# A message ring of 19 pairs filled from the last score on, fewer statistics operations per pair, group 2 normalised inside the sums, two limit loads for four

## The reference

```python
h = relu(layernorm(x))
x_src, x_dst = h @ W_src.T, h @ W_dst.T
alpha = sum(x_src[src] * att_src[type]) + sum(x_dst[dst] * att_dst[type])   # per edge and head, self loops of type 0 added
alpha = where(alpha >= 0, alpha, 0.2 * alpha)
a = exp(alpha - segment_max(alpha, dst)[dst])
a = a / segment_sum(a, dst)[dst] * edge_weight
out = segment_sum(x_src[src] * a, dst) + bias
g = layernorm(out + h) * ln1_g + ln1_b
ff = gelu(g @ ffn_W1.T + ffn_b1) @ ffn_W2.T + ffn_b2
return x + layernorm(g + ff) * ln2_g + ln2_b
```

## Time and profile before

| | us |
|---|---|
| median of 3 runs | 3229.35 (3222.22 to 3236.22) |
| the profiled execution | 3217.3 |
| its span, first to last instruction | 3215.6 |

### The profile page before, as it was taken

The page is one execution under the profiler, slowest core; times in us unless marked ns, Lnnn a source line. Parts: engine busy times, 40 slices in busy tenths (PEclk is TensorE's granted clock), DMA queues, the critical chain, the costliest instruction groups (busy, mean ns, idle before and its releaser), DMA issues.

```text
span 3215.6 us, 56979 instructions
## 1 busy us (share of the span) xinstructions
PE 2992.1 (93%) x19965; PEld 2730.3 (85%) x19965; DVE 2254.3 (70%) x6326; ACT 1802.3 (56%) x3372; POOL 1729.2 (54%) x1493
## 2 busy tenths in 40 slices
PE   4887365999999999999999999999999999999998
PEld 4776344999999998999999999999999999999997
DVE  6888654777777776777777767777777777777775
ACT  4676243555555555555555555555555555555554
POOL 5665654555555555555555555555555555555552
PEclk9999687999999999999999999999999999999999
DMA  4446283222111222222222222221211122222210
GB/s 153 139 146 132 64 234 85 60 60 58 54 55 58 59 59 59 60 60 60 60 60 60 60 60 60 60 58 55 56 57 58 58 58 60 60 60 60 60 47 27
DMA packets 86991, 228.73 MB, mean 71 GB/s; under 512 B 19367, under 2 KB 23501, under 8 KB 86706
## 3 DMA queue, kind: packets, MB, share of 16 engines
q1 hardware_dynamic: 53810, 145.86, 13.3%
q0 software_dynamic: 31664, 78.07, 11.6%
q10 hardware_dynamic: 1232, 1.15, 0.1%
HBM read 146.85 MB, written 78.20 MB: 70 GB/s over the span
## 4 chain that ended last, share of the span: by engine, by line
PE 81%; DVE 1%; POOL 1%; issue 1%; ACT 1%; DMA 0%; DVEq 0%; POOLq 0%; ACTq 0%
PE ps_f L1324 33%; PE ps_a L1339 12%; PE ps_a L1341 11%; PE ps_a L1340 11%; PE ps_x L1361 8%; PE ps_t L1371 3%; PE ps_t L1349 3%; ACT h L715 0%; DVE arena L1129 0%; DVE act_lo L1189 0%; POOL arena L610 0%; POOL n_rstd L586 0%; ACT ps_f L740 0%; DMA arena<-sums,node_rows 0%; DVE arena L1155 0%
## 5 line engine op out<-in xcount | busy, mean ns | idle before, releaser
L1189 DVE TENSOR_TENSOR act_lo<-ps_f,act_hi 128x512 fp32r<-128x512 f32 x784 | 539.2, 688 | 742.6 <-ACT ps_f L740 742.3
L739 ACT ACTIVATE act_hi<-ps_f,hidden_bias 128x512 fp32r<-128x512 f32 x784 | 537.0, 685 | 863.6 <-PE ps_f L1324 863.6
L1339 PE MATMUL ps_a<-ffn_hi,act_hi 128*128 128x256 f32 x3136 | 900.5, 287 | 2.8 <-DVE arena L1155 2.7
L1341 PE MATMUL ps_a<-ffn_hi,act_lo 128*128 128x256 f32 x3136 | 887.5, 283 | 0.0
L1340 PE MATMUL ps_a<-ffn_lo,act_hi 128*128 128x256 f32 x3136 | 884.7, 282 | 0.0
L1324 PE MATMUL ps_f<-zt_hi,ffn_hi 128*128 128x512 f32 x1568 | 617.9, 394 | 11.6 <-DVE act_lo L1189 9.9
L1339 PEld LDWEIGHTS ps_a<-ffn_hi,act_hi 128*128 128x128 f32 x3136 | 591.5, 189 | 31.4 <-issue 4.5
L1324 PE MATMUL ps_f<-zt_lo,ffn_hi 128*128 128x512 f32 x1568 | 616.9, 393 | 0.0
L1324 PE MATMUL ps_f<-zt_hi,ffn_lo 128*128 128x512 f32 x1568 | 616.9, 393 | 0.0
L1340 PEld LDWEIGHTS ps_a<-ffn_lo,act_hi 128*128 128x128 f32 x3136 | 591.0, 188 | 24.1
L1341 PEld LDWEIGHTS ps_a<-ffn_hi,act_lo 128*128 128x128 f32 x3136 | 590.9, 188 | 0.0
(11 more groups left out here) (230 smaller groups left out, 5436.3 us busy)
## 6 DMA issues: line engine op xcount, KB each, us to landing
xb<-in_x SPq DMA_DIRECT2D x98, 512.0 KB, 5.9
out<-arena SPq DMA_DIRECT2D x98, 512.0 KB, 5.0
msgs<-arena SPq DMA_DIRECT2D x49, 256.0 KB
arena<-msgs SPq DMA_DIRECT2D x49, 256.0 KB, 4.7
sums<-arena SPq DMA_DIRECT2D x49, 256.0 KB, 3.9
arena<-sums,node_rows POOLq DMA_INDIRECT x392, 3.7
xb<-in_x,arena POOLq DMA_INDIRECT x196, 2.8
arena<-in_w_t SPq DMA_DIRECT2D x2, 1024.0 KB, 7.5
```

What stands on the lines that cost most here:

```text
L739: act.activation(act_hi[:, m % AB, :], ps_f[:, m % 2, :], ACT.Gelu, bias=hidden_bias[:, m:m + 1]).then_inc(act_hi_ready, 1)
L1189: dve.tensor_tensor(act_lo[:, m % AB, :], ps_f[:, m % 2, :], act_hi[:, m % AB, :].bitcast(F32), ALU.subtract).then_inc(act_lo_ready, 1)
L1339: pe.matmul(to, act_hi[:, m % AB, cols], ffn2[0][:, m, :], start=(m == 0 and t % 2 == 0), stop=False, skip_group_check=True)
L1341: ins = pe.matmul(to, act_lo[:, m % AB, cols], ffn2[0][:, m, :], start=False, stop=(m == MF - 1), skip_group_check=True)
```

## The change

1. `front_stats`: the two DVE operations that made var + EPS and -mean are gone. The square root takes EPS as its bias, `front_rstd` adds EPS and turns the sign inside operations that were there. mv has four slots.
2. The ring in which messages wait for their store is MB = 4 pairs, not two.
3. The ring of messages loaded back is SB = 19 pairs, not 4. Four of its slots (SBN) are a place of their own; the other 15 (msg_late) lie over the scores' parts, base and the stored messages. SP issues 4 loads behind the last message store, 15 more when alpha_ready is there and all messages are stored, and then one per pair as its slot comes free.
4. Node groups: input_stats(0) stands in pair 47, input_stats(1) behind alpha_ready, input_stats(2) in pair 12 of the sums. n_var and n_mm have two slots. POOL's input_rstd of groups 0, 1 and 2 stands ahead of c = 8, 20 and 84. ACT's relu of group 2 stands in the sums, behind the equals of pair 26.
5. ACT issues a gelu of one column that nobody reads behind the Exp.
6. Fix: one load each from SP and ACT, first and last rows of half the chunks. POOL loads the node rows only when the first record is made (they lie elsewhere now).

The core of the diff:

```diff
-SB = 4
+MB = 4
+SB = 19
+SBN = 4
...
-RSTD_AT = (16, 24)
+RSTD_AT = (8, 20, 84)
+STATS2_AT = 12
+RELU2_AT = 26
...
-        assert (RB - 1) * NT <= NCH * SC
-        other_rows = src_sc.rearrange("p c s -> p (c s)")[:, 0:(RB - 1) * NT].bitcast(I32).rearrange("p (b t) -> p b t", b=RB - 1)
-        msg_out = part([2, 2, D])
+        msg_out = part([MB, 2, D])
...
+        msg_late = arena[:, edges_end:edges_end + (SB - SBN) * 2 * D].rearrange("p (a b) -> p a b", b=D)
+        assert edges_end + (SB - SBN) * 2 * D <= used[0]
...
-        fix_a, fix_b, fix_rec = (prob[:, 2 * n:2 * n + 2, :].rearrange("p h e -> p (h e)") for n in range(3))
+        fix_ends = prob[:, 0:4, :].rearrange("p (a h) e -> p a (h e)", a=2)
+        fix_rec = prob[:, 4:6, :].rearrange("p h e -> p (h e)")
+        other_rows = prob[:, 6:2 * HEADS, :].rearrange("p h e -> p (h e)")[:, 0:(RB - 1) * NT].bitcast(I32).rearrange("p (b t) -> p b t", b=RB - 1)
...
-        msg_in = part([2 * SB, D])
+        msg_soon = part([2 * SBN, D])
...
             return [sem(f"{name}_{i}") for i in range(2)]
-        msg_stored, rec_in, stored = (sem_pair(n) for n in ("msg_stored", "rec_in", "stored"))
+        rec_in, stored = (sem_pair(n) for n in ("rec_in", "stored"))
+        msg_stored = [sem(f"msg_stored_{i}") for i in range(MB)]
...
         rows_stored = [sem(f"rows_stored_{i}") for i in range(RB)]
...
                 eng.wait_ge(agg_stored[i], 16 * ((NPAIR + RO - 1 - i) // RO))
-        def sums_rows(p, c):
-            return sums[0:EP].rearrange("(j p c) d -> p c j d", p=P, c=2)[p, c]
+        def loaded(j):
+            b = j.off % SB
+            return msg_soon[:, 2 * b:2 * b + 2, :] if b < SBN else msg_late[:, 2 * (b - SBN):2 * (b - SBN) + 2, :]
+        def load_ends(eng, c):
+            eng.dma_start(fix_ends[c:NCH:2, :, :], sums[0:EP].rearrange("(j p c) d -> c j p d", p=P, c=2)[c][:, 0:P:P - 1, :]).then_inc(fix_in, 16)
         def node_buf(g):
...
+            wait_count(eng, x_stats, TG * f.n)
...
-                eng.bn_aggr(mv[:, f.par, t, :], stat[:, t, :]).then_inc(x_stats, 1)
-            eng.wait_ge(x_stats, TG * f.n + TG)
-            eng.tensor_scalar(vareps[:, f.off % 4, :], mv[:, f.par, :, 1], EPS, None, ALU.add).then_inc(x_prepared, 1)
-            eng.tensor_scalar(minus_mean[:, f.off % 4, :], mv[:, f.par, :, 0], -1.0, None,
-                              ALU.mult).then_inc(x_prepared, 1)
+                eng.bn_aggr(mv[:, f.off % 4, t, :], stat[:, t, :]).then_inc(x_stats, 1)
...
-            eng.wait_ge(x_prepared, 2 * (2 * q + pairs))
-            eng.activation(root[:, at, :], vareps[:, at, :], ACT.Sqrt).then_inc(x_root, 1)
+            eng.wait_ge(x_stats, TG * (2 * q + pairs))
+            eng.activation(root[:, at, :], mv[:, at, :, 1], ACT.Sqrt, bias=eps[:, :], scale=1.0).then_inc(x_root, 1)
...
-            eng.tensor_tensor(vareps[:, at, :], vareps[:, at, :], rstd[:, at, :], ALU.mult).then_inc(x_pow, 1)
+            eng.scalar_tensor_tensor(out=newton[:, at, :], in0=mv[:, at, :, 1], scalar=EPS, in1=rstd[:, at, :],
+                                     op0=ALU.add, op1=ALU.mult).then_inc(x_pow, 1)
...
-            eng.scalar_tensor_tensor(out=rstd[:, at, :], in0=vareps[:, at, :], scalar=1.5, in1=root[:, at, :],
+            eng.scalar_tensor_tensor(out=rstd[:, at, :], in0=newton[:, at, :], scalar=1.5, in1=root[:, at, :],
...
-            eng.tensor_tensor(shift[:, at, :], minus_mean[:, at, :], rstd[:, at, :], ALU.mult).then_inc(x_scaled, 1)
+            eng.scalar_tensor_tensor(out=shift[:, at, :], in0=mv[:, at, :, 0], scalar=-1.0, in1=rstd[:, at, :],
+                                     op0=ALU.mult, op1=ALU.mult).then_inc(x_scaled, 1)
...
                 sp.dma_start(msgs.rearrange("(j p c) d -> j p c d", p=P, c=2)[j.n],
-                             msg_out[:, j.par, :, :]).then_inc(msg_stored[j.par], 16)
+                             msg_out[:, j.off % MB, :, :]).then_inc(msg_stored[j.off % MB], 16)
...
             steps(sp, pair, 0, NPAIR, *PAIR_LOOP)
-            sp.wait_ge(msg_stored[0], 16 * ((NPAIR + 1) // 2))
-            sp.wait_ge(msg_stored[1], 16 * (NPAIR // 2))
...
                 b = j.off % SB
+                if j.n < SBN:
+                    sp.wait_ge(msg_stored[j.n % MB], 16 * (j.n // MB + 1))
+                if j.n == SBN:
+                    sp.wait_ge(alpha_ready, 1)
+                    for i in range(MB):
+                        sp.wait_ge(msg_stored[i], 16 * ((NPAIR + MB - 1 - i) // MB))
                 wait_count(sp, agg_done, j.n + 1 - SB)
-                sp.dma_start(msg_in[:, 2 * b:2 * b + 2, :], msgs.rearrange("(j p c) d -> j p c d", p=P, c=2)[j.n]).then_inc(msg_loaded[b], 16)
+                sp.dma_start(loaded(j), msgs.rearrange("(j p c) d -> j p c d", p=P, c=2)[j.n]).then_inc(msg_loaded[b], 16)
             def sum_pair(j):
-                load_pair(j + 3)
+                load_pair(j + SB - 1)
...
                                  rec_out[:, 2 * (j.off % RO):2 * (j.off % RO) + 2, :]).then_inc(agg_stored[j.off % RO], 16)
-            steps(sp, sum_pair, -3, NPAIR, *SUM_LOOP)
+            steps(sp, sum_pair, 1 - SB, NPAIR, *SUM_LOOP)
             def nodes(i):
...
             records_stored(sp)
-            for c in range(2):
-                sp.dma_start(fix_a[c:NCH:2, :], sums_rows(0, c)).then_inc(fix_in, 16)
+            load_ends(sp, 0)
...
             if NG > 1:
...
                 wait_count(pool, nh_ready, TG * (g.n - 1))
-                pool.tensor_tensor(n_rstd[:, g.par, :], n_var[:, :], minus_half[:, 0:TG], ALU.pow).then_inc(n_pow, 1)
+                pool.tensor_tensor(n_rstd[:, g.par, :], n_var[:, g.par, :], minus_half[:, 0:TG], ALU.pow).then_inc(n_pow, 1)
                 pool.wait_ge(n_pow, g.n + 1)
-                pool.tensor_tensor(n_shift[:, g.par, :], n_mm[:, :], n_rstd[:, g.par, :], ALU.mult).then_inc(n_scaled, 1)
+                pool.tensor_tensor(n_shift[:, g.par, :], n_mm[:, g.par, :], n_rstd[:, g.par, :], ALU.mult).then_inc(n_scaled, 1)
...
                 gather(j)
...
                 pool.wait_ge(rows_stored[i], 16 * ((NCH + RB - 1 - i) // RB))
-            pool.wait_ge(alpha_ready, 1)
+            pool.wait_ge(rec_made, 1)
...
                 pool.dma_start(to, of[0:NROWS, :].rearrange("(p t) o -> p (t o)", p=P)).then_inc(node_rows_in, 16)
...
                     first_residual(n)
-                if g.exists(NG):
+                if g.exists(NG) and g.n > 2:
                     input_rstd(g)
-            pool.wait_ge(rec_made, 1)
...
             pool.wait_ge(empty_stored, 16)
...
+            act.wait_ge(consts, 13)
...
             act.activation(prob[0:NCH], prob[0:NCH], ACT.Exp).then_inc(exp_ready, 1)
+            act.activation(unread[:, :], ones[:, :], ACT.Gelu)
...
                 act.wait_ge(line_turned, j.n + 1)
...
                 for m in range(MF):
-                    if m == 0 and front and on:
+                    if m == 0 and front and a.n > 2:
...
                         first_norm(n)
...
                     input_hi(Step(0, TURN_AT.index(j.n - 1), 4))
+                if j.n == RELU2_AT:
+                    input_relu(Step(0, 2, 4))
...
             records_stored(act)
-            for c in range(2):
-                act.dma_start(fix_b[c:NCH:2, :], sums_rows(P - 1, c)).then_inc(fix_in, 16)
+            load_ends(act, 1)
             steps(act, nodes, -1, NG, *NODE_LOOP)
...
                 src = ps_f if j.par == 0 else ps_a
-                wait_count(dve, msg_stored[j.par], 16 * j.half)
+                wait_count(dve, msg_stored[j.off % MB], 16 * j.before(MB))
...
                 for q in range(2):
-                    dve.scalar_tensor_tensor(out=msg_out[:, j.par, q, :], in0=src[:, q, 0:D], scalar=ew[:, 2 * j.n + q:2 * j.n + q + 1],
+                    dve.scalar_tensor_tensor(out=msg_out[:, j.off % MB, q, :], in0=src[:, q, 0:D], scalar=ew[:, 2 * j.n + q:2 * j.n + q + 1],
...
             def input_stats(g):
...
                 dve.wait_ge(n_stats, 2 * TG * g.n + 2 * TG)
-                wait_count(dve, n_scaled, g.n)
-                dve.tensor_scalar(n_var[:, :], n_mv[:, :, 1], EPS, None, ALU.add).then_inc(n_prepared, 1)
-                dve.tensor_scalar(n_mm[:, :], n_mv[:, :, 0], -1.0, None, ALU.mult).then_inc(n_prepared, 1)
+                wait_count(dve, n_scaled, g.n - 1)
+                dve.tensor_scalar(n_var[:, g.par, :], n_mv[:, :, 1], EPS, None, ALU.add).then_inc(n_prepared, 1)
+                dve.tensor_scalar(n_mm[:, g.par, :], n_mv[:, :, 0], -1.0, None, ALU.mult).then_inc(n_prepared, 1)
...
                     front_stats(dve, j + 3)
-                if j.n >= NPAIR - 2:
-                    input_stats(Step(0, j.n - (NPAIR - 2), 4))
+                if j.n == NPAIR - 2:
+                    input_stats(Step(0, 0, 4))
...
                 if j.n % 2 == 0 and (j + 2).exists(NPAIR):
...
             dve.sem_inc(alpha_ready, 1)
+            input_stats(Step(0, 1, 4))
             ticks = [0]
...
```

(14 more changed lines are left out.)

## The result

The changed kernel took 3216.79 us (median of 20 runs, 3208.55 to 3223.55), the kernel before 3228.93 (median of 20 beside them, 3222.22 to 3236.22): a ratio of 0.9963, 95% interval 0.9956 to 0.9971, or -12.1 us. The gain is real and lies inside the half per cent that the text calls no change. The forecast was -29 us.

The account below looks back on a forecast made before the run. Only the first 537 us could gain, bound by no single engine but by waits, two of them on POOL's 98 scatters. -18.8 - 1.2 - 9 = -29 us from 3229.35 gives 3200, range 3176 to 3218.

Parts of the forecast that it names:

- Statistics per pair: Front loop: two DVE operations fewer in each of 49 pairs; -2 us, bounds 0 and -4, mostly vanishing behind waits on POOL.
- The last pairs: End of the front loop: two DVE waits and a PE gap go; scores end 15.4 us earlier, at 321.
- From the scores to the sums: ACT's relu of group 1 still waits for POOL at c = 20; sums start 8 us earlier, at 373.5.
- The first 27 pairs: Sums: 19 pairs loaded ahead, 1.56 to 2.2 us per pair; ACT comes to j = 26 between 416 and 432.
- The gate at c = 84: Sums: ACT's relu of group 2 waits for POOL's rstd, c = 84 at 437.5; last record 475.3, -18.8 us.
- The fix: Behind the last record: two limit loads for four, one issue less on each queue; -1.2 us, bounds 0 and -1.5.
- the cover of the node rows: Before the fix: c = 97 at 455, node rows back by 466 to 470, ahead of 481; cover 11 us.
- Into the node loop: Fix to first gelu: relu of group 2 and table load out of the way; -9 us, bounds -7 and -10.5.
- both gates are late: Rival: scatters 3.2 us each until c = 20, c = 84 near 449; -17, 3212; chance 0.20 together with prefetch idle.
- The point from which the change is slower: Rival of a slower kernel: c = 84 at 466.5, 1.88 us per scatter from c = 20; chance 0.06 including unchanged.

Follow-up runs that it names:

- a1: The changed kernel run and profiled again, unedited, beside the kernel before: median 3205.70 us, -11.6 us to before, ratio 0.9963.
- e9: The changed kernel with a ring of 5 pairs for loading back instead of 19, rstd(2) still ahead of c = 84: 3201.33 us, ratio 0.995 to before.
- e5: The changed kernel with group 2 normalised in the node loop again, the gelu behind the Exp kept: 3196.31 us, ratio 0.9944 to before.
- e10: The changed kernel with a ring of 5 pairs and rstd ahead of c = 8, 10 and 60: 3186.63 us, ratio 0.9904 to before.
- e1b: The changed kernel with input_rstd of group 2 ahead of c = 60 instead of 84: 3186.42 us, ratio 0.9916 to before.
- after: The changed kernel itself in its first profile: profiled execution 3220.57 us, span 3218.7; median of its 20 runs 3216.79 us.
- e4: The changed kernel with rstd ahead of c = 8, 10 and 60 and the 15 bulk loads held until the Exp: 3193.89 us, ratio 0.9937 to before.
- set 2: One of five sets of runs, each on one chip; it held a1, e1b, e4 and e5, and the kernel before took 3217.30 us there.
- b0: The kernel before, unchanged, run and profiled again in set 1: 3329.63 us, ratio 1.0033 to the kernel before beside it.
- b1: The kernel before, unchanged, run and profiled again in set 3: 3303.74 us, ratio 0.9967 to the kernel before beside it.

## Why the prediction was wrong

The total. Against the profiled execution before, which is of another set, a1's span is 11.0 us shorter: last record -0.5, fix -1.1, into the node loop -7.9, node loop -1.5 (2679.8 to 2678.3). Forecast: -18.8, -1.2, -9, 0. One term fell.

**Statistics per pair, right.** DVE's busy time from 40 to 200 us went from 134.95 to 128.75, while the first scatter, behind the last gather, goes out 1.8 us earlier (293.4 to 291.6; 4.1 in the first profile). -2 was forecast, bounds 0 and -4. Runs whose front loop is the same (e9, e5) have it 4.6 and 2.1 earlier, so the size is not surer than that.

**The last pairs, right.** -15.4 forecast, -17.2 in a1 (336.5 to 319.3).

**From the scores to the sums, half wrong.** The place of the wait was right: ACT's relu of group 1 at c = 20. The scatters took 2.8 us each from c = 8 instead of 2.2, so c = 20 came at 350.0 and not 346.4. The first record is 4.8 us earlier, where 8 were forecast. The rows held the hint: 3.2 us beside only four loads. The text took 2.2 for the window as if the burst were over in part of it. The landings show that it isn't: median 10.8 us in a1 from 322 to 344 (five landings, 7.1 to 11.2) and a single one of 14.4 in the first profile, against 7.3 beside four loads, which is a single one too; in e10, with 5 loads, three landings took 5.7 to 6.3. Here stood the Trainium skill (DMA: Bandwidth & Descriptors, Queues, rings and completion order), by whose round over the queues packet by packet a deep queue should hold a scatter up no more than a shallow one. The traces speak against it: 5.7 to 7.3 us beside 4 or 5 loads, up to 11.2 and 14.4 beside 19. They are few landings, and e1b, also with 19 loads, has 5.5 to 9.4.

**The first 27 pairs, right.** ACT came to pair 26 at 453.36 - 27.52 = 425.8, forecast 416 to 432; records 0 to 26 took 48.2 us, 1.86 each, between 1.56 and 2.2. The prefetch works as planned, and it runs into the gate.

**The gate at c = 84, right in kind, wrong in size: this is the term that failed.** c = 84 was put at 437.5 and came at 453.9, 16.4 us late. 3.6 of them are c = 20. c = 20 to 41 was taken at 1.27 us each behind rstd(1) and took 30.3 us instead of 27.1: 3.2 more. c = 41 to 84 was put at 64 us, 35 scatters at the old sums' 1.55 and 8 at 1.27, and took 73.5, 1.71 each: 9.5 more. While the pairs ran, c = 41 to 64, it was 1.94 each. The 1.55 came from sums that loaded with DMA engines at 0.76 from 381 to 440 us; in a1 they were at 0.92 there, and landings took 6.9 us at the median instead of 5.1. The stretches from 381 to 440 us, before and a1:

```profile
381.00:440.00 59.00, 42.31 (x188) 32.66 (x187) 34.42 (x54) 30.55 (x82) 39.12 (x38) 0.86 0.76 197
```

```profile
381.00:440.00 59.00, 36.48 (x193) 28.30 (x191) 37.25 (x66) 29.02 (x77) 33.25 (x34) 0.93 0.92 241
```

And the landings of the scatters, before from 381 to 465 us, a1 from 381 to 425:

```profile
DMA to landing us min/median/max: 3.4/5.1/7.2
```

```profile
DMA to landing us min/median/max: 5.4/6.9/7.9
```

A pace read at a DMA share of 0.76 was carried to one of 0.92. Other runs bear it out: while the pairs run, the scatters take 1.80 us each in e1b and 1.76 in e9, at shares of 0.99 and 0.97. The last record came 18.3 us late. 14.4 of them stand at the end of the relu (455.4, forecast 441), 2 less than at c = 84, because rstd(2) stands ahead of that scatter and the sum put it behind. The other 3.9 are the pace behind the gate: 22 pairs in 38.2 us, 1.74 each and not 1.56.

So the quicker pairs, with their loads and stores denser, made the gate later (this is read from the traces; no run slowed the pairs alone), and c = 20 to 84 took 103.8 us in a1 against 102.3 before, although the pairs stood still for 27.5 of them. e1b shows what the gate cost, 19.3 us against a1; the forecast missed by 17.4 (29 - 11.6).

**The fix, not told by these runs.** 7.48 to 6.33 us in a1, -1.2 forecast; but with the same two loads the wait is 6.6 to 8.4 us in e9, after, e10, e1b, e5 and e4, so the agreement may be luck. The remark that the cover of the node rows is thin holds: c = 97 went out at 471.8, 17 us later than the text had it, which the late sums hid, and in e1b, e4, e5 and e10, without the gate, that wait of 13.4, 16.0, 11.8 and 12.5 us is what ends last ahead of the fix.

**Into the node loop, right.** 24.2 us from the fix to the first gelu instead of 32.1: -7.9, forecast -9, bounds -7 and -10.5. PE is what is late: its first hidden block ran at the lower of its two levels, 1.2 GHz. Matmuls of that block, before and a1, from timelines of PE:

```profile
525.96 0.39 PE L1324 MATMUL ps_f<-zt_hi,ffn_hi 128*128 128x512 f32 x1
```

```profile
524.78 0.63 PE L1342 MATMUL ps_f<-zt_hi,ffn_hi 128*128 128x512 f32 x1
```

The granted clock was 0.64 from 513 to 525 us in a1 and 0.77 from 515 to 527 before, with PE as busy in both (8.0 and 7.9 us); why it was lower wasn't tried. From the block's first matmul to its input for the gelu it took 2.8 us instead of 1.7, which is the 1.1 us that the -9 lacked. In the table load the row was right: in the first profile it starts as the Exp ends and takes 1.28 us, and e5, where the load is gone but the relu stays, is 1.0 us quicker there. The drain of the Trainium skill (ScalarE: Activation LUTs, What ACT_TABLE_LOAD costs) would have made it 2.66.

**The rivals.** Nearest was that both gates are late (c = 84 near 449, 3212). It still took c = 84 too early; c = 20, put at 355, came at 350.0 and 354.4. Its "sums from 375.5" doesn't follow: with c = 20 at 355 the forecast's own steps give 382, and the first profile has the first record 0.5 us ahead of the old one. The point from which the change is slower was put a little too late: c = 84 at 466.5 by the text; the first profile had it at 464.9, with a span already 3.1 us longer than before. Between the two profiles of the changed kernel c = 84 moves by 11.0 us and the span by 14.1. But they are of two sets, whose medians lie 11.1 us apart, so how much of the spread of the times comes from this queue is not shown.

## What to carry to other kernels

When a step that others wait for stands at a place in a long queue of small transfers, price that queue at the load that the change makes, not at the one of the trace, and put the step as far ahead as its inputs allow: ahead of c = 60 instead of 84 was worth 19 us in set 2, more than all the rest there. Before counting a prefetch as a gain, find where the time that it frees goes: with 5 pairs in the ring instead of 19 the kernel was no slower, and the scatters that everything waited for went out earlier. And when a gate is taken away, look for the end of the same queue behind it: of 38 us at the records 19 reached the end.

## What the runs showed of the hardware

- The landing of a scatter of 128 numbers of 4 bytes depends on what else the DMA engines carry: 2.1 us with the sums at rest, medians of 5.1 to 6.9 in the sums, 7.3 (one landing) beside four loads of 256 KB, a median of 10.8 in a1 and one of 14.4 in the first profile beside nineteen. Among the last gathers of the front loop, at a DMA share of 0.99 from 300 to 316 us in a1, four landings took 7.8 to 17.3 us with no such load. With four in flight a quarter of it bounds the pace: 10.8 / 4 = 2.7, where 2.8 was measured.
- One and the same kernel took 3217 to 3229 us (medians) in some sets and 3318 to 3328 in others, with the node loop alike (PE bound) and what lies ahead of it 108 to 112 us longer in the profiles of b0 and b1. The cause is open; the same chip number stands at a quick and at a slow set.
- Loads and stores of the sums together reached 281 GB/s with the DMA engines at 0.99 once no gate stood in their way (e1b, 381 to 440 us; PE was busy for 48.6 of those 59 us). That a faster version would meet this share next is a guess that no run tried.
